# Width-one attention: queries and keys on all 128 partitions, the bound folded, and its steps at other groups

## The reference

```python
qkv = jnp.einsum('bnc,fc->bnf', x, w_qkv)          # f = 3 * 64
q, k, v = jnp.split(qkv, 3, axis=-1)                # each (b, n, 64): a head has one number per token
dots = jnp.einsum('bhid,bhjd->bhij', q, k) * scale  # d = 1: an outer product of q and k
dots = jnp.where(causal, dots, -jnp.inf)
attn = jax.nn.softmax(dots, axis=-1)
out = jnp.einsum('bhij,bhjd->bhid', attn, v)
return jnp.einsum('bnh,ch->bnc', out, w_out)
```

## Time and profile before

| what | value |
|---|---|
| median of three runs | 3169.06 us (3167.29, 3169.06, 3172.32) |
| profiled execution, own time | 3174.21 us |
| its span in the trace | 3172.4 us |
| mean granted TensorE clock | 0.967 of full speed |
| TensorE busy | 2943.1 us, 93% |
| VectorE busy | 1863.2 us, 59% |
| ScalarE busy | 1253.7 us, 40% |

### The profile page before, as it was taken

The page is one execution under the profiler, slowest core; times in us unless marked ns, Lnnn a source line. Parts: engine busy times, 40 slices in busy tenths (PEclk is TensorE's granted clock), DMA queues, the critical chain, the costliest instruction groups (busy, mean ns, idle before and its releaser), DMA issues.

```text
span 3172.4 us, 52215 instructions
## 1 busy us (share of the span) xinstructions
PE 2943.1 (93%) x20631; PEld 1958.4 (62%) x20671; DVE 1863.2 (59%) x6438; ACT 1253.7 (40%) x1944; POOL 432.8 (14%) x458
## 2 busy tenths in 40 slices
PE   7999999988989889988998899999999999998998
PEld 4666666865555556655655556566667766766653
DVE  5534443699999537775677788584343344434455
ACT  2222221335656433324443578554232333323443
POOL 0010010114343311000000256310000000000000
PEclk9999999998999999999999799899999999998999
DMA  3000000010000100000000111100000000000000
GB/s 129 1 1 0 1 0 1 1 52 1 2 1 2 34 32 1 1 5 1 2 1 1 27 36 26 44 2 27 1 1 1 1 1 1 1 1 9 2 1 27
DMA packets 22028, 37.75 MB, mean 12 GB/s; under 512 B 2132, under 2 KB 19733, under 8 KB 20760
## 3 DMA queue, kind: packets, MB, share of 16 engines
q1 hardware_dynamic: 20968, 34.02, 3.2%
q10 hardware_dynamic: 816, 0.39, 0.1%
HBM read 26.81 MB, written 2.10 MB: 9 GB/s over the span
## 4 chain that ended last, share of the span: by engine, by line
PE 77%; DVE 16%; ACT 4%; issue 2%; DMA 0%; DVEq 0%; SPq 0%; POOL 0%; ACTq 0%; POOLq 0%
PE ps L415 45%; DVE arena L568 4%; PE ps L620 2%; PE ps L3040 2%; PE ps L3059 2%; PE ps L686 2%; PE ps L516 2%; ACT arena L674 2%; PE ps L2356 2%; PE ps L1590 2%; PE ps L2310 2%; PE ps L727 2%; DVE arena L1924 2%; PE ps L2913 1%; PE ps L553 1%
## 5 line engine op out<-in xcount | busy, mean ns | idle before, releaser
L415 PE MATMUL ps<-weights,arena 128*128 128x256 f32 (+4 forms) x2480 | 696.1, 430 | 38.9 <-DVE arena L1805 23.5
L415 PEld LDWEIGHTS ps<-weights,arena 128*128 128x128 f32 (+1 forms) x2480 | 462.8, 196 | 204.0 <-issue 94.3
L415 PE MATMUL ps<-arena,weights 128*128 128x256 f32 (+4 forms) x1726 | 560.4, 473 | 14.5 <-DMA weights<-in_w_L_attn 5.8
L415 PEld LDWEIGHTS ps<-arena,weights 128*128 128x128 f32 (+1 forms) x1726 | 316.7, 191 | 217.7 <-issue 154.0
L415 PE MATMUL ps<-arena 128*128 128x256 f32 (+4 forms) x1618 | 429.1, 418 | 6.0 <-ACT arena L4758 1.5
L415 PEld LDWEIGHTS ps<-arena 128*128 128x128 f32 (+2 forms) x1618 | 300.1, 189 | 115.6 <-issue 74.9
L568 DVE TENSOR_REDUCE arena<-ps 128x16 f32<-128x1232 f32 (+2 forms) x96 | 179.1, 1865 | 145.4 <-PE ps L546 48.0
L674 ACT ACTIVATE arena<-ps 77x2048 f32<-77x2048 f32 (+1 forms) x112 | 210.0, 1875 | 120.2 <-PE ps L620 58.4
L1924 DVE MATCH_REPLACE8 arena<-arena 128x77 f32<-128x77 f32 x1024 | 214.3, 224 | 0.0
L2323 ACT ACTIVATE arena<-ps 128x1536 f32<-128x1536 f32 x128 | 185.7, 1451 | 56.6 <-PE ps L2312 49.7
L855 POOL TENSOR_TENSOR x<-x,weights 128x512 f32<-128x512 f32 x32 | 43.8, 1370 | 1201.0 <-DVE arena L821 1153.3
(11 more groups left out here) (427 smaller groups left out, 4421.5 us busy)
## 6 DMA issues: line engine op xcount, KB each, us to landing
arena<-arena SPq DMA_DIRECT2D x156, 32.0 KB
weights<-in_w_L_ffn SPq DMA_DIRECT2D x1, 3848.0 KB, 11.6
weights<-in_w_L_attn SPq DMA_DIRECT2D x1, 3840.0 KB, 14.8
weights<-in_w_L_xattn SPq DMA_DIRECT2D x3, 1024.0 KB, 6.3
weights<-in_w_L_ffn SPq DMA_DIRECT2D x1, 3072.0 KB, 9.9
x<-in_x SPq DMA_DIRECT2D x2, 1024.0 KB
weights<-in_w_L_xattn SPq DMA_DIRECT2D x1, 2048.0 KB, 7.5
out<-x SPq DMA_DIRECT2D x8, 256.0 KB, 2.2
```

Of the source, the lines that this page charges most:

```text
L415: ins = k.nc.tensor.matmul(out, lhsT, rhs, start=start and i == 0, stop=i == n - 1)
```

## The change

Queries come to lie on partitions 0 to 63 and keys on 64 to 127 of the same 256 columns, where both lay on partitions 0 to 63 side by side. For batches 0 to 4 (`n < APART`) two 64-column products write the two halves, for batches 5 to 7 one product of 128 columns writes both. The copy out of PSUM, the three-way split and its buffers then work on 128 partitions and half as many columns. The bound is folded: its first 128 columns lie on the lower partitions and its last 128 on the upper, so its minimum is two instructions and each part of it is sent by two transfers, the lower half with the queries and the upper half with the keys (24 transfers a batch instead of 21). `kmax` and `kmin` have buffers of their own. `BOUND_AT` goes from (9, 10, 13, 13, 14) to (9, 13, 13, 14, 15); the places for batches 0 and 1 stay.

```diff
-ROWS_DMAS = 2 * PAIRS + PARTS
+ROWS_DMAS = 2 * PAIRS + 2 * PARTS
...
-            qkm=c.take(3, SEQ), rest=c.take(3, SEQ), v=[c.take(2, NH1) for _ in two], seen=c.take(P),
+            qkm=c.take(SEQ + P), rest=c.take(SEQ + P), kmax=c.take(SEQ), kmin=c.take(SEQ), gap=c.take(832),
+            v=[c.take(2, NH1) for _ in two], seen=c.take(P),
...
 def rows_of_part(k, s, eng, n, i, queues):
...
+    q, key = s.parts[0:NH1, i, 0:SEQ], s.parts[NH1:P, i, 0:SEQ]
...
         if "k" in queues:
-            eng.dma_start(krows[PARTS * i + j:P:PAD, :, :], part[:, 1, :]).then_inc(rows, 16)
+            eng.dma_start(krows[PARTS * i + j:P:PAD, :, :], key).then_inc(rows, 16)
         if "q" in queues:
-            eng.dma_start(qrows[PARTS * j + i:P:PAD, :, :], part[:, 0, :]).then_inc(rows, 16)
-    if "q" in queues:
-        eng.dma_start(qrows[PAIRS + i:P:PAD, :, :], part[:, 2, :]).then_inc(rows, 16)
+            eng.dma_start(qrows[PARTS * j + i:P:PAD, :, :], q).then_inc(rows, 16)
+    for half in (0, 1):
+        if "qk"[half] in queues:
+            eng.dma_start(qrows[PAIRS + i:P:PAD, :, half * P:(half + 1) * P],
+                          s.parts[half * NH1:(half + 1) * NH1, i, SEQ:SEQ + P]).then_inc(rows, 16)
...
 def step_qk_tensor(k, pe, s, n, b):
-    for i in (0, 1):
-        ins = proj_feature(k, k.ps[0:NH1, b, i * SEQ:(i + 1) * SEQ], w_of(k, s.stage, "wqkv", KC), s.zT[n % 2],
-                           i * NH1, NH1)
+    w, wide = w_of(k, s.stage, "wqkv", KC), NH1 if n < APART else P
+    for at in range(0, P, wide):
+        ins = proj_feature(k, k.ps[at:at + wide, b, 0:SEQ], w, s.zT[n % 2], at, wide)
...
 def step_qk_vector(k, dve, s, n, b):
-    v.tensor_copy(s.qkm[0:NH1, 0:2, :], cut(k.ps[0:NH1, b, :], c=2)).then_inc(*s.sig.up("qk"))
+    v.tensor_copy(s.qkm[:, 0:SEQ], k.ps[:, b, 0:SEQ]).then_inc(*s.sig.up("qk"))
...
 def step_bound_vector(k, dve, s, n, i):
-    q, key, out = (s.qkm[0:NH1, j, :] for j in range(3))
+    q, key = s.qkm[0:NH1, 0:SEQ], s.qkm[NH1:P, 0:SEQ]
...
-        v.tensor_tensor(out, kmax, kmin, ALU.min).then_inc(*done)
+        for half in (0, 1):
+            at = slice(half * P, (half + 1) * P)
+            ins = v.tensor_tensor(s.qkm[half * NH1:(half + 1) * NH1, SEQ:SEQ + P], kmax[:, at], kmin[:, at], ALU.min)
+        ins.then_inc(*done)
...
 def step_split_vector(k, dve, s, n, i):
-    x, rest, parts = s.qkm[0:NH1], s.rest[0:NH1], s.parts[0:NH1]
+    x, rest, parts = s.qkm, s.rest, s.parts
...
-BOUND_AT = (9, 10, 13, 13, 14)
+APART = 5
+BOUND_AT = (9, 13, 13, 14, 15)
```

More of the change, by code:

```diff
@@ L2241, in width_one_plan @@
     two = (0, 1)
-    s = Bag(stage=st, z=c.take(2, D), zT=[c.take(KC, SEQ) for _ in two], parts=c.take(PARTS, 3, SEQ, dt=BF16),
-            qkm=c.take(3, SEQ), rest=c.take(3, SEQ), v=[c.take(2, NH1) for _ in two], seen=c.take(P),
+    s = Bag(stage=st, z=c.take(2, D), zT=[c.take(KC, SEQ) for _ in two], parts=c.take(PARTS, SEQ + P, dt=BF16),
+            qkm=c.take(SEQ + P), rest=c.take(SEQ + P), kmax=c.take(SEQ), kmin=c.take(SEQ), gap=c.take(832),
+            v=[c.take(2, NH1) for _ in two], seen=c.take(P),
             krows=[c.take(16, SEQ, dt=BF16) for _ in two],
@@ L2249, in width_one_plan @@
     assert low.at <= HALF, low.at
-    s.kmax, s.kmin = s.rest[:, 0, :], s.rest[:, 1, :]
     s.sig = Signals(k.signals, st, B, 1, z=1, zT_ps=1, zT=1, qk_ps=1, qk=1, v_ps=1, v=1, put=2, parts=PARTS, s_ps=GROUPS,
@@ L2272, in rows_of_part @@
     rows = s.moved.sems["rows"][0]
-    part, qrows, krows = s.parts[0:NH1, i], s.qrows[n % 2], s.krows[n % 2]
+    qrows, krows = s.qrows[n % 2], s.krows[n % 2]
+    q, key = s.parts[0:NH1, i, 0:SEQ], s.parts[NH1:P, i, 0:SEQ]
     eng.wait_ge(*s.sig.at("parts", 0, n, i + 1))
@@ L2486, in step_qk_scalar @@
     act.wait_ge(*s.sig.at("qk_ps", 0, n, 1))
-    k.nc.scalar.activation(s.qkm[0:NH1, 0:2, :], cut(k.ps[0:NH1, b, :], c=2), ACT.Copy).then_inc(*s.sig.up("qk"))
+    k.nc.scalar.activation(s.qkm[:, 0:SEQ], k.ps[:, b, 0:SEQ], ACT.Copy).then_inc(*s.sig.up("qk"))
 def step_v_scalar(k, act, s, n, b):
```

## The result

The changed kernel takes 3226.27 us (median of six executions, 3189.98 to 3235.36) against 3170.64 us for the kernel before on the same chip (six, 3167.29 to 3175.44). The ratio is 1.0148, 95% interval 1.0107 to 1.0189. The prediction of 3162.2 us is 64 us too low and its range ended at 3171. The profiled execution took 3227.84 us, span 3225.9.

A forecast was written before the change was run, and what follows sets the result against it. Steady batches were taken as bound by TensorE, with VectorE ending some waits in batches 0 to 2 and the hand-over. Gains of 3.7 + 1.0 + 0.4 + 1.2 + 0.6 = 6.9 us took 3169.06 to 3162.2 us, range 3155 to 3171.

The forecast's parts named there:

- The clock stays low longer: Rival: batch 1's shorter query and key product may fail to restore full clock; 13 us more, 3175 us, chance 0.12.
- Two products side by side: Batches 0 to 4: 64-column products on different output partitions overlap, 0.95 us at full clock; batch 4's product saves 0.9 us.
- rival of program order: Matmuls start and end in order, so two halves need seven steps for eight; gain only 4.9 us, 3164.2 us, chance 0.2.
- Steady batches, 29.4 us: Batches 3 to 5, bound by TensorE: one 128-column product saves 0.94 us each, 2.8 us in all.
- batch 2: Batch 4's product, made here, saves 0.9 us; shorter VectorE splits give back 0.6 us of mask waits (0 to 0.7).
- VectorE's splits near half: Five split operations on half the columns go from some 5.0 to about 2.5 us; worth 0 in steady batches.
- Hand-over and batch 0 to 1: Product and splits at the previous stage's end gain 1.0 us (-0.4 to 1.8); batch 0 to 1 gains 0.4 (0.3 to 0.9).
- such a wait: Sign of a wrong forecast: a first score of a batch that waits for rows sent by DMA.
- early gains are swallowed: Rival: in batches 0 to 2 and the hand-over VectorE or ScalarE is late anyway; only 3.7 us remain, 3165.4, chance 0.13.
- Batch 1, 1.2 us: Batch 3's product, made here, 0.9 us shorter and the copy behind it 0.3: 1.2 us gained, between 0.5 and 2.1.
- DMAs: 24 transfers a batch for 21 stay hidden, some 10 us to spare; batch 0's extra issues hold ScalarE up 0.4 us.
- The sum: Gains of 3.7 + 1.0 + 0.4 + 1.2 + 0.6 = 6.9 us over the stage, for a median of 3162.2 us.

The follow-up runs named there:

- One kernel with the old preparation, the last above: Kernel before, long product kept; VectorE's rounding operations moved behind batch 1's first mask, second scan of batch 1's bound behind the reciprocal: 3188.49 us, ratio 1.0030.

## Why the prediction was wrong, point by point

- **The clock stays low longer** (chance 0.12, 3175 us) is what happened, by the mechanism named: groups do not bring the clock back, the long product did. The forecast's own sum had no term for the clock, and that is the step of it that failed. The rival had one, and two of its steps failed. Its price, 13 us, let the half clock run on only to "the next products between groups that are as dense", some twelve groups. What stands there is the product for the next batch's values (1856.93), and neither it nor the output product ever brought the full clock back, 0 of 40; the next query and key product is a batch on, the short one did so 10 times in 20, and each that fails costs a batch, 53.3 - 29.4 = 23.9 us. And it took the low stretch of 1808 us as the only one at stake: I used the gap of 1.17 us as one "that cost no clock", a property of the gap. By the nine observations it belonged to the gap and the long product ahead of it. Added to the 3162.2 of the forecast, one lost batch gives 3186 and three give 3234 (estimates), both far over the range's top of 3171; the changed kernel's own executions run from 3190 to 3235.
- **The argument against that rival**, that as many multiplications are done "only closer together", was wrong: closer together they are over sooner, and the short ones succeeded 10 times in 20, the longer ones 11 times in 12.
- **Two products side by side**: right. 1.09 us at full clock and 1.98 at half (forecast 0.95 and 1.85); the single product of 128 columns takes 1.13 (forecast 0.94). The rival of program order (seven steps for eight) would have needed some 1.65 at full clock (seven eighths of 1.88); it is out.
- **Steady batches, 29.4 us**: right (29.44 in batch 5). With the clock kept, batch 2 is right too. The kernel with one product doubled shows both, in its batches 2 and 3; by first scores they take 30.25 and 29.44 us, 1.53 and 0.81 less than before (forecast 1.5 and 0.94):

```profile
1844.60:1874.80 30.20, 29.39 (x413) 18.43 (x412) 25.53 (x61) 24.45 (x20) 16.80 (x17) 1.00 0.22 68
1874.80:1904.20 29.40, 29.27 (x409) 18.64 (x408) 23.11 (x38) 24.46 (x20) 18.03 (x17) 1.00 0.10 26
```

- **VectorE's splits near half**: mis-sized. Lines by form of the changed kernel, from 1752 to 2090 us (count, busy, mean ns), and two of them in its timeline at the hand-over:

```profile
L2588 DVE TENSOR_TENSOR arena<-arena 128x384 f32<-128x384 f32 x7 | 6.9, 990 | 0.0
...
L2567 DVE TENSOR_TENSOR arena<-arena 64x128 f32<-64x128 f32 x14 | 6.1, 435 | 0.2
L2582 DVE TENSOR_TENSOR arena<-arena 128x384 f32<-128x384 f32 x7 | 5.6, 803 | 0.0
...
L2579 DVE CAST arena<-arena 128x384 bf16<-128x384 f32 x7 | 4.7, 668 | 0.0
...
L2545 DVE COPY arena<-ps 128x256 f32<-128x256 f32 x6 | 2.5, 418 | 0.0
```

```profile
1739.05 0.36 DVE L2579 CAST arena<-arena 128x384 bf16<-128x384 f32 x1
1739.44 0.56 DVE L2582 TENSOR_TENSOR arena<-arena 128x384 f32<-128x384 f32 x1
```

  The five means sum to 3.73 us (668 + 803 + 603 + 990 + 670) for 5.0, not 2.5; the copy is 0.42 (forecast 0.35); the minimum as two is 0.87 for 0.71. The same two in the timeline of the kernel before, at full size:

```profile
1743.38 0.55 DVE L2573 CAST arena<-arena 64x768 bf16<-64x768 f32 x1
1743.96 0.95 DVE L2576 TENSOR_TENSOR arena<-arena 64x768 f32<-64x768 f32 x1
```

  So even there, where they are fastest, they shrink to 0.65 and 0.59 of what they were, not to half. It cost nothing in steady batches, as forecast.
- **Hand-over and batch 0 to 1**: right in one execution for the hand-over, not in the others, and swallowed behind it. The two rows, of the changed kernel:

```profile
1752.39 0.37 PE L2313 MATMUL ps<-arena 32*128 32x256 bf16 x1 [2.09 <-DMA arena<-arena]
...
1760.37 1.11 PE L727 MATMUL ps<-ident,arena 128*128 128x128 f32 x4 [1.81 <-DVE arena L720]
```

  Measured from the product at 1715.50 (1720.13 before, so 4.63 us to be added), TensorE restarts at 1765.00, 0.85 earlier than in the earlier trace rows; I had 1.0. But the first score waits 2.09 us for the rows and is no earlier (1757.02 for 1757.12). I had listed such a wait as a sign of error, and had overlooked that it was there before, with 1.27 us. In the ten further profiled executions that have the folded preparation this wait is 4.5 to 5.4 us; counted from the same product, the first score comes 0.8 to 1.7 us later than before and the restart up to 1.0 later. One kernel with the old preparation, the last above, waited 3.22 us there and was 0.6 late at the first score, so how much of this is the change's stays open; the gain of 1.0 us is not borne out. And the first mask of batch 1 lets TensorE on at 1803.12 + 4.63 = 1807.75, where the earlier trace rows has 1807.81. So of the 1.4 us that I gave to both places 0.06 was left: there the rival "early gains are swallowed" was right. The gap grew from 1.75 to 2.95 as TensorE came earlier to the same mask. (The low stretch of batch 0 was 23.9 us long here for 20.5, which works against the gain too.)
- **Batch 1, 1.2 us**: right up to the drop. From that mask to the means it is 1833.83 - 1803.12 = 30.71 us, for 31.81 before, 1.10 less.
- **DMAs**: right in the steady batches, where no first score waits for rows.
- **The sum** without the clock looks right and is so by luck. The kernel doubled for batch 3 alone has all of the change and one microsecond more, and is 7.5 us faster in the median (interval from 13.0 faster to 0.3 slower); I had 6.9. But the terms as measured are 3 x 0.81 + 1.53 + 1.10 + 0.06 = 5.1 us, and in the profiled execution of that kernel batches 0 to 5 took 207.6 us for 210.3 before, only 2.7 less: batch 1, with the second copy and a low stretch of 23.9 us for 20.5, took 45.81 for 44.18.

## What to carry to other kernels

Before a dense piece of TensorE work is shortened, see in the trace whether a low stretch of the clock ends in it; if so, it may be what gives back the full clock to everything behind it until the next such piece, and the loss is to be priced per piece (here 24 us each), not per group. A gap that costs no clock in one profile is no safe gap once the work ahead of it changes. Here, making the shortened piece twice for batch 3 alone cost 1 us of TensorE and gave back some 53, though one of twelve executions was still slow at 3201.87.

## What the runs showed of the hardware that I had not expected

- TensorE at half clock for 143.4 us without any idle time that the profile shows, and for 180.9 us with 1.1 us of it at the start, on groups of 32-row scores and 32-column values.
- Two halves of 64 columns, one chain of four records behind the other in the program, on different output partitions: 1.09 us, as fast as one product of 128 columns (1.13) and not the 1.95 of the two on the same partitions.
- The same kernel on the same chip spreads over 45 us (3190 to 3235), and time and mean granted clock go together (3189.98 us at 0.961, 3235.36 at 0.945).
- The same split operation takes 0.36 us at the hand-over and 0.67 on average in the stage (and 0.56 against 0.80 for the subtraction). GpSimd does its masks in the stage and stood idle at the hand-over; whether that is the reason was not tried.
- Still open: why a short product succeeds in one batch and fails in the next, with the same work around it. The runs show how often, not what decides.
